# 32-row score tiles, one value product per token tile, and other engines for normalising and for the scaled output, in a two-layer decoder

## The reference, cut to what matters

```python
q = q.reshape(b, s, N_HEADS, HEAD_DIM).transpose(0, 2, 1, 3)      # 32 heads of 16
scores = jnp.einsum('bhqd,bhkd->bhqk', q, k) / np.sqrt(HEAD_DIM)
attn = jax.nn.softmax(scores, axis=-1)
out = jnp.einsum('bhqk,bhkd->bhqd', attn, v)
out = out.transpose(0, 2, 1, 3).reshape(b, s, HIDDEN)
return bitnet_linear(out, o_weight, o_scale)     # layer 0: y = (x @ sign(w)) * per-column scale
```

## Time and profile before

| | us |
|---|---|
| median of 3 runs (lowest, highest) | 2255.3 (2254.97, 2259.81) |
| the profiled execution | 2255.08 |
| its span, first to last instruction | 2253.3 |
| outside the span in that execution | 1.8 |

### The profile page before, as it was taken

One profiled execution on the slowest core, in us unless ns is written; L12 is line 12 of the kernel. 1 busy time (PEld: TensorE's weight loads), 2 busy tenths in 40 slices (PEclk: granted clock), 3 DMA queues, 4 the chain that ended last, 5 costly groups with the idle time before them and its releaser, 6 DMA issues. The chain is left out here.

```text
span 2253.3 us, 39463 instructions
## 1 busy us (share of the span) xinstructions
PE 2185.9 (97%) x15918; PEld 1736.1 (77%) x15918; DVE 1368.5 (61%) x2383; ACT 1016.5 (45%) x1734; POOL 886.7 (39%) x659
## 2 busy tenths in 40 slices
PE   6997999999999999999999999999999999999998
PEld 4775878778787787877878777888887777777776
DVE  6887534343333453334333548797795888888866
ACT  6774543445435454354543552111102666666532
POOL 2675231432414423143241345221122768777611
PEclk9999999999999999999999999999999999999999
DMA  4000111110112101111010113000002000100002
GB/s 165 2 20 21 57 39 38 38 57 19 38 38 75 57 20 38 38 38 57 20 38 36 43 59 102 1 0 0 0 1 75 20 1 28 36 26 11 2 1 75
DMA packets 23032, 80.65 MB, mean 36 GB/s; under 512 B 4048, under 2 KB 6224, under 8 KB 16720
## 3 DMA queue, kind: packets, MB, share of 16 engines
q1 hardware_dynamic: 22864, 78.28, 10.2%
HBM read 74.08 MB, written 4.19 MB: 35 GB/s over the span
## 5 line engine op out<-in xcount | busy, mean ns | idle before, releaser
L2570 PE MATMUL xat_TP<-shared_rounded 128*128 128x512 f32 x1024 | 322.6, 396 | 5.8 <-issue 5.8
L2244 POOL TENSOR_TENSOR xat_T<-xat_T,xat_mask 128x512 f32<-128x512 f32 x64 | 81.7, 1299 | 514.3 <-DVE xat_T L2334 514.3
L104 PE MATMUL xat_G<-xat_xnT_hi,shared_rounded 128*128 128x512 f32 x768 | 244.4, 391 | 0.0
L2231 POOL TENSOR_TENSOR shared_rounded<-shared_landing,shared_rounded 128x2048 fp32r<-128x2048 f32 x39 | 179.4, 4607 | 153.4 <-ACT shared_rounded L2088 153.4
L2570 PEld LDWEIGHTS xat_TP<-shared_rounded 128*128 128x128 f32 x1024 | 187.2, 188 | 58.2 <-issue 22.4
L2361 DVE TENSOR_TENSOR X<-X,xat_TP 128x512 f32<-128x512 f32 x128 | 86.9, 679 | 198.5 <-PE xat_TP L2570 198.5
L2570 PE MATMUL xat_TP<-shared_rounded,xat_oT_lo 128*128 128x512 f32 x512 | 199.9, 390 | 0.0
L2325 DVE RECIPROCAL xat_q_inv_rms<-xat_OT 128x16 f32<-128x16 f32 x32 | 8.3, 260 | 312.7 <-PE xat_OT L2497 312.7
L104 PE MATMUL ffn_H<-shared_rounded 128*128 128x448 f32 (+1 forms) x816 | 179.1, 368 | 3.2 <-DVE ffn_h_kept L1397 1.9
L1329 POOL TENSOR_TENSOR ffn_one_hot<-ffn_one_hot,ffn_block_rank 128x448 f32<-128x448 f32 x64 | 75.5, 1180 | 253.4 <-DVE ffn_one_hot L1378 253.4
L687 POOL TENSOR_TENSOR two_T<-two_T,two_row_max 128x512 f32<-128x512 f32 x128 | 131.5, 1049 | 103.2 <-DVE two_row_max L778 102.9
(11 more groups left out here) (359 smaller groups left out, 5021.7 us busy)
## 6 DMA issues: line engine op xcount, KB each, us to landing
shared_landing<-in_Cq_q SPq DMA_DIRECT2D x16, 1024.0 KB, 4.9
shared_landing<-in_Cq_o SPq DMA_DIRECT2D x16, 1024.0 KB, 4.8
shared_landing<-in_Cq_kv SPq DMA_DIRECT2D x8, 1024.0 KB, 6.9
shared_landing<-in_ctxT_paired SPq DMA_DIRECT2D x4, 1024.0 KB, 6.9
two_ctxT_raw<-in_ctxT SPq DMA_DIRECT2D x8, 512.0 KB, 3.8
shared_landing<-in_w1T SPq DMA_DIRECT2D x8, 448.0 KB, 3.8
shared_landing<-in_w SPq DMA_DIRECT2D x7, 512.0 KB, 3.6
out<-X SPq DMA_DIRECT2D x6, 512.0 KB, 3.0
```

The source lines that it names most:

```text
L104: last = eng.matmul(out, a, b, start=(n == 0), stop=(n == len(steps) - 1))
L2231: return eng.tensor_tensor(w[1][:, :, :], landed[:, :, :], w[0][:, :, :].bitcast(F32), ALU.subtract)
L2244: eng.tensor_tensor(T[:, n, :, :], T[:, n, :, :], mask[:, :].unsqueeze(1).to_broadcast([P, ROWS, SEQ]), ALU.add)\
L2570: last = eng.matmul(TP[m % 2][:, :], x, w, start=(n == 0), stop=(n == len(steps) - 1))
```

## The change

Six edits, all inside `small_attention` and its helpers.

1. `scores` contracts over 32 rows instead of 64. A matmul gives two heads, 128 columns, in one of eight positions (four row groups q, two sequences b); there are 16 for each slot instead of 8. The scores of both slots of a tile are made at once in the even slot (32 matmuls) and fill all four banks of S, one bank for each row group; slots 0 and 1 of a call are made apart. The wait is now for the reading of the slot just before.
2. `values` is done once a tile, in odd slots, with 256 columns instead of twice with 128. `keep_PT` of the first half in an odd slot waits for it.
3. In the second call ACT normalises the rows of groups 2 to 8 (`scalar_xn`: 28 activations with a scale and a bias for each row), in slots 6 and 7, in place of DVE; DVE makes the bias with one small instruction a group and inverts the root at the head of slot 6.
4. In the first call ACT copies the output product out of PSUM, and POOL multiplies it by the scales and then adds it to X, with two buffers `ysc`; DVE has no part in it.
5. q3 moves to part a of slot 7, y0 to its part b, since all four q are wanted in slot 0 now.
6. The order of the heads in the bias table and in the views follows the banks.

The core of the diff:

```diff
+    def scalar_xn(self, eng, i, t):
+        if t == 0:
+            eng.wait_ge(self.stat.sem, self.stat.at(i, self.inverse))
+            eng.wait_ge(self.turned.sem, self.turned.before(i))
+        eng.activation(self.xn[:, t, :], x_tile(self.X, i, t), ACT.Identity, bias=self.sd[:, t:t + 1],
+                       scale=self.rstd[:, t:t + 1]).then_inc(self.xn_ready.sem, 1)
...
+                elif name[0] == "y" and sign:
+                    t = int(name[1])
+                    eng.wait_ge(y_done.sem, y_done.at(i, t + 1))
...
+                    eng.activation(ysc[t % 2], bank[:, :], ACT.Copy).then_inc(y_kept.sem, 1)
...
                 if u >= PTS:
-                    eng.wait_ge(pv_done.sem, pv_done.at(0, (u - PTS) // 2 + 1))
+                    eng.wait_ge(pv_done.sem, pv_done.at(0, (u - PTS) // PTS + 1))
...
+                    eng.wait_ge(y_kept.sem, y_kept.at(i, t + 1))
+                    eng.tensor_tensor(yt, yt, osc[:, :], ALU.mult).then_inc(y_added.sem, 1)
                     eng.wait_ge(y_added.sem, y_added.at(i, 2 * t + 1))
                     xt = x_tile(X, i, t)
-                    eng.tensor_tensor(xt, xt, ysc, ALU.add).then_inc(y_added.sem, 1)
+                    eng.tensor_tensor(xt, xt, yt, ALU.add).then_inc(y_added.sem, 1)
...
-                if s >= 2:
+                if s >= 1:
                     free = sub_ready if sign else s_read
-                    eng.wait_ge(free.sem, free.at(0, 2 * (s - 2) + 2))
-                for cc in range(2):
+                    eng.wait_ge(free.sem, free.at(0, 2 * s))
+                for c in chunks:
                     for b in range(2):
-                        for r in range(2):
-                            rows = slice(r * SEQ, (r + 1) * SEQ)
+                        for q in range(4):
+                            r, g = divmod(q, 2)
+                            rows = slice(q * 2 * HD, (q + 1) * 2 * HD)
                             tok = t * P + b * SEQ
-                            at = r * D + cc * 4 * SEQ
+                            at = g * D + c * 2 * SEQ
...
-            b[4], b[5], a[6], b[6], b[7] = [(j, "vt")], [(j, "q1")], [(j, "vp")], [(j, "q2")], [(j, "q3")]
+            b[4], b[5], a[6], b[6], a[7] = [(j, "vt")], [(j, "q1")], [(j, "vp")], [(j, "q2")], [(j, "q3")]
             if not late:
-                a[7] = [(i, "y0")]
+                b[7] = [(i, "y0")]
```

More of the change, by code:

```diff
@@ L661, in _ @@
                     weight_hi(0, f"o{s - 1}")
+                for i in range(2, NG + 1 if pair else 0):
+                    for t in norm_slots(i).get(s, ()):
+                        ln.scalar_xn(eng, i, t)
                 for g, name in weight_slots(s):
@@ L880, in _ @@
                             take(item)
+                for i in range(2, NG + 1 if pair else 0):
+                    if 0 in norm_slots(i).get(s, ()):
+                        ln.vector_inverse(eng, i)
                 if s < LASTP:
@@ L922, in _ @@
                             ln.vector_inverse(eng, i)
[L923 removed]
+                        elif not sign and i > NG:
                             ln.vector_xn(eng, i, t)
```

116 lines of the change are left out of this document (68 added, 48 removed).

## The result

The changed kernel takes 2240.7 us (median of 4 runs, 2238.8 to 2241.2), the one before 2255.1 in the same comparison: a ratio of 0.9932, 95% interval 0.992 to 0.9944. It is 14.5 us faster; 38 were forecast. The time lies inside the stated range of 2208 to 2248, in its upper fifth, and outside the forecast's own of 2209 to 2227: six tenths of the expected gain are missing, and this part is about where they are.

What follows compares the result with a forecast made beforehand. TensorE was taken to set the pace, VectorE close behind and setting the first call's last group. Gains of 11.6 + 17 + 11.4 = 40, less 2 for the clock, took 2255.3 to 2217 us; own range 2209 to 2227, stated 2208 to 2248.

Steps and rivals of the forecast that it cites:

- Eight abreast, a tile of 2.04 us: TensorE, per tile: eight score positions run at once, scores 1.04 us plus values 1.0, 2.04 instead of 3.20.
- four abreast (1.9): Rival, scores block: only four passes run at once, scores 1.9 us, a tile 2.9, total 2247; chance 14%.
- a floor (2.5): Rival, scores block: every pass takes at least 36 ns, scores 2.5 us, a tile 3.5, total 2267; chance 6%.
- Groups 4 to 7, 4.2 each: Second call, followed by cross groups with k from the context: full 4.64 us saved less 0.4 for POOL, 17 in all.
- First groups of both calls, 2.9 each: Group 1 of each call: 2.9 us gained from k on, VectorE covering the relief before k.
- First call, groups 2 and 3: 3.5 us gained each: 2.9 from k on plus 0.6 for VectorE's dropped multiplication; periods near 41 us.
- Group 4, 2.5 gained: First call's last group, set by VectorE: 1 us gained for two tiles, little for the others, 2.5 in all.
- The tail, 1.25 longer for the last y: First call's end: copy, multiplication and addition on ACT and POOL delay the next stage's start; net 1 us lost.
- Group 8, 2.9: Second call's last group, followed by the expert part's products from the same rows: 2.9 us gained.
- The clock, 2 us taken off: Allowance in the sum for TensorE's clock: 2 us off the gain of 40, leaving 38.
- The rival: New waits before k in seven groups each bring a half-clock stretch, 12 us, some 3 more elsewhere: 2232; chance 20%.
- The row edit costs nothing: Second call, slots 6 and 7: ACT's 28 normalisations, 2.6 us a group, fit its 19 idle; VectorE falls to about 42.

## Why the prediction was right or wrong

The step that failed is the one from TensorE's relief to time, the terms 11.6 + 17 + 11.4 = 40 of the prediction's sum. It counted the wait before k as nearly the only new one and the groups of each call as alike but for the last of the first. In its own terms: the first call, 11.4, measured -0.6; groups 1, 2, 3 and 8 of the second call, 11.6, measured 4.1; groups 4 to 7, 17, measured 12.3; the stages between, nothing, measured -1.7. What the runs showed in its place are waits for buffers and banks that other engines free late, and half-clock stretches behind some of them:

- **Eight abreast, a tile of 2.04 us: right.** Measured 1.14 and 1.0, 2.14. Over 48 tiles the 0.1 is 5 us of TensorE's time. The rivals of four abreast (1.9) and of a floor (2.5) are out; so is the Trainium skill's 60 cycles a matmul (TensorEngine Tiling (Array Packing), section Instruction Overhead) as a price: the estimate by it was 1.6 us, and 64 passes took 1.14.
- **Second call, steady groups: right where VectorE's part was drawn in.** 49.6 and 50.0 us against 49.4 forecast. The wait is split, 1.0 before x3 and 0.4 before k, where 1.7 before k was forecast.
- **Groups 4 to 7, 4.2 each: the step that failed is "there the full 4.64 counts".** VectorE doesn't bind by the rest of the rows alone: its addition of y1 frees the bank of x3, and TensorE waits 1.0 us for it in groups 4, 5 and 7 whatever k comes from. Measured 2.9, 1.5, 5.0 and 2.9, 3.1 on average; leaving out one maximum shortened all of them but group 6. In group 5 three waits for ScalarE's copies of turned probabilities stand besides (0.68, 0.80 and 0.86 us; before, 0.22 and 0.81); group 6 keeps TensorE's whole relief, 4.3 us, and stands 0.6 less than before. Groups of kind cross take 49.0 to 51.2 us, not 47.9.
- **First groups of both calls, 2.9 each: failed, 7.6 us.** The prediction counted them as steady groups and passed over the one order in them that the change moves, slot 1's scores behind vt's product. Undone, 2.9 of the 4.0 missing in the second call's come back, 1.2 of them by way of the clock; in the first call's 0.7. There three waits for ScalarE's copies of turned probabilities remain (0.73, 0.87 and 1.37 us) where the kernel before has none over 0.4; the second of them is the wait for the value block told below, the other two are copies behind ScalarE's other work.
- **First call, groups 2 and 3: 42.0 and 41.5 for "near 41": near in size, for a wrong reason, so in part by luck.** The output edit was priced at 0.6 us a group for a multiplication less. Its move shows as 1.4 and 1.5, of which 0.4 each is standing and the rest a half-clock stretch avoided; its second buffer, which the prediction did not price at all, is worth 6 us over the call. Without that buffer the new tiles lose in the first call.
- **Group 4, 2.5 gained: failed, and with the tail the largest miss, 6.5 us.** The prediction checked VectorE's and GpSimd's sums for a tile (9 and 9.3 us) but not the ring of PT, though point 2 of the change names its wait: with values once a tile, the copy that overwrites the first buffer waits for the value block. It saw the 0.78 us behind value blocks and counted it once, in the tail. Freed, group and tail give back 5.8 us, with GpSimd next late, in one tile by 3.6 us. The move of y to slower engines costs 2.4 there as well, of which the tail's 1.25 was counted.
- **The tail, 1.25 longer for the last y: right to the hundredth.** The wait before the next stage is 3.92 instead of 2.67.
- **Group 8, 2.9: failed.** It was taken as a steady group because its rows feed the expert part. Its VectorE carries that part's normalisations too, and the earlier trace rows had no stretch of it. Two statistics moved win back 2.5 to 2.9 us, 1.2 of it in the wait and the rest with the half-clock stretch behind it, which the kernel before had too (2156.6).
- **The clock, 2 us taken off: undersized.** Five more halved stretches than before, 20.5 us more at half clock. The rival gave it 12 us in the second call's groups; there, inside the steady ones, none came, at waits of 1.03 and 0.38, but its first group has one, which the prediction had ruled out. The others came in the last group of the first call and at the next stage's start. The rival's 2232 was nearer than the forecast's 2217, but for another place; 2247, of the rival that the scores block rules out, was nearer still, by luck.
- **The row edit costs nothing: right**, but "without this, slots 6 and 7 would get close" was not where it told: it brings 1.3 us, in one group, in TensorE's waits before the turns of x.

## What to carry to other kernels

When a change makes the bounding engine faster, list who frees each buffer and bank that it asks for, and not only each engine's sum per tile: a ring as long as one batch ties the producer to the consumer as soon as the consumer works batchwise. Price the steady groups and the edges (first group, last group, hand-over to the next stage) apart, each from its own stretch; here the edges held two thirds of what was missed. And ask of an edit that moves work between engines whom the waiting engine then waits for: the moved 0.66 us gained 1.4 us in one group, mostly through the clock, and lost in another, and the buffer that came with it was worth more than the move.

## What was unexpected of the hardware

Eight 32-row positions begin 6.6 ns apart and run abreast; a round of eight at 128 columns takes 0.11 us. From the 37th pass on the starts spread to about 16 ns each (starts in the trace of the block at 1789.29), so a block of 64 takes 1.14 us and not 1.04, and one of 128 takes 2.03, 13.9 ns for each further pass. Why they spread is not shown. A granted clock of half, 1.2 of 2.4 GHz, came in stretches of 3.4 to 10.2 us, and which stand draws one can't be told by the stand's length: 2.67 us before the next stage went without in one kernel and with in another, 2.10 us without in two and with in two; in the first call's last group pairs of 0.80 and 1.07 us and one of 0.35 and 1.47 went without, pairs of 0.87 and 1.48 with.
